# Gated attention with a routed mixture of experts: the expert table read along the pairs, first loads and transposes in front of the last attention products, three waits among GpSimd's last scatters

## The reference, cut to what matters

```python
x = L0_attn_x                       # 8 batches, 512 rows, 256 columns, float32
xn = _layernorm(x, axis=-1)
# attention over channels: scores are 256 x 256 per batch, summed over the 512 rows
scores = jnp.einsum('bes,bfs->bef', qT, kT) / np.sqrt(HEAD_DIM)
s = swapaxes(einsum(softmax(scores), vT)) @ Wo
# experts: 32, of 8 groups; the best 3 groups, in them the best 6 experts of each row
scores = jax.nn.softmax(xn @ gate_weight.T)
topk_weight, topk_idx = jax.lax.top_k(tmp_scores, TOP_K)      # TOP_K = 6
h = jax.nn.silu(xn @ w1[e].T) * (xn @ w3[e].T)                # for each expert e
y = sum over the chosen e of weight * (h @ w2[e].T)
shared = jax.nn.silu(xn @ sw1.T) * (xn @ sw3.T) @ sw2.T       # one expert for all rows
g = _silu(y + shared)
return x + s * g
```

## Time and profile before

| | |
|---|---|
| median of 3 runs | 695.25 us (692.28 to 696.24) |
| profiled execution, and its span | 693.48 us, 691.7 us |
| TensorE products busy | 543.7 us, 79% of the span |
| TensorE weight loads busy | 449.3 us, 65% |
| VectorE busy | 472.7 us, 68% |
| ScalarE busy | 357.0 us, 52% |
| GpSimd busy | 379.7 us, 55% |
| DMA | 174.80 MB, mean 253 GB/s |
| chain that ended last | DVE 32%, PE 27%, issue 18%, unknown queue 14% |

### The profile page before, as it was taken

The page is one execution under the profiler, slowest core; times in us unless marked ns, Lnnn a source line. Parts: engine busy times, 40 slices in busy tenths (PEclk is TensorE's granted clock), DMA queues, the critical chain, the costliest instruction groups (busy, mean ns, idle before and its releaser), DMA issues.

```text
span 691.7 us, 14479 instructions
## 1 busy us (share of the span) xinstructions
PE 543.7 (79%) x4095; PEld 449.3 (65%) x4095; DVE 472.7 (68%) x1443; ACT 357.0 (52%) x606; POOL 379.7 (55%) x402
## 2 busy tenths in 40 slices
PE   8778895979696859628999987878888788888840
PEld 7555774756565647427999776777767777677730
DVE  7966886888786848742454566767667677676767
ACT  5535573747464534324656554655646556465531
POOL 1275666766666667671003565656556565565664
PEclk9888997999998989777999999999999999999975
DMA  9999994949492523653998888998888889988765
GB/s 322 413 355 354 348 352 146 350 166 353 168 330 103 194 92 122 209 178 97 194 216 268 285 270 261 290 292 269 277 267 287 290 262 287 284 274 272 236 200 174
DMA packets 111288, 174.80 MB, mean 253 GB/s; under 512 B 25072, under 2 KB 68848, under 8 KB 110320
## 3 DMA queue, kind: packets, MB, share of 16 engines
q1 hardware_dynamic: 87280, 108.29, 47.9%
q0 software_dynamic: 18432, 50.36, 23.6%
q10 hardware_dynamic: 5504, 15.24, 6.2%
HBM read 78.41 MB, written 92.27 MB: 247 GB/s over the span
## 4 chain that ended last, share of the span: by engine, by line
DVE 32%; PE 27%; issue 18%; another core or an unknown queue 14%; ACT 7%; DVEq 1%; DMA 1%; ACTq 0%
DVE sw L1149 8%; PE ps L851 8%; PE ps L726 4%; PE ps L742 4%; DVE work L1175 3%; PE ps L873 3%; DVE w_all L1066 2%; DVE work L1168 2%; PE ps L748 2%; DVE early L1157 2%; PE ps L734 2%; PE ps L834 2%; DVE pad L1175 2%; ACT w_all L574 1%
## 5 line engine op out<-in xcount | busy, mean ns | idle before, releaser
L524 POOL DMA_INDIRECT early<-slots_d,slot_at x192 | 183.5, 956 | 186.6 <-remote 80.0
L503 POOL DMA_INDIRECT slots_d<-early,slot_at x96 | 97.5, 1015 | 70.9 <-issue 25.7
L503 POOL DMA_INDIRECT slots_d<-work,slot_at x96 | 96.5, 1006 | 45.8 <-issue 25.6
L663 ACT ACTIVATE xnT<-ps 128x1024 f16<-128x1024 f16 x67 | 68.9, 1029 | 86.0 <-remote 61.5
L834 PE MATMUL ps<-ident,work 128*128 128x128 f16 x796 | 70.6, 221 | 51.7 <-issue 51.6
L851 PE MATMUL ps<-w_all,xnT 128*128 x798 | 101.4, 276 | 3.6 <-issue 2.8
L834 PEld LDWEIGHTS ps<-ident,work 128*128 128x128 f16 x796 | 56.3, 99 | 58.8 <-issue 55.4
L851 PEld LDWEIGHTS ps<-w_all,xnT 128*128 128x128 f16 x798 | 73.4, 98 | 18.4 <-issue 8.1
L1175 DVE CAST work<-ps 128x256 f16<-128x256 f32 x75 | 31.7, 422 | 75.8 <-remote 53.3
L1149 DVE SCALAR_TENSOR_TENSOR sw<-early,wk,sw 128x256 f32<-128x256 f32 x160 | 77.8, 486 | 3.5
L684 ACT ACTIVATE early<-ps 128x512 f32<-128x512 f32 x112 | 67.9, 607 | 20.8 <-PE ps L873 10.7
(11 more groups left out here) (164 smaller groups left out, 968.2 us busy)
## 6 DMA issues: line engine op xcount, KB each, us to landing
slots_d<-early SPq DMA_DIRECT2D x112, 256.0 KB
work<-slots_d SPq DMA_DIRECT2D x100, 256.0 KB
slots_d<-pad SPq DMA_DIRECT2D x7, 3072.0 KB
w_all<-in_wexp ACTq DMA_DIRECT2D x7, 1536.0 KB
slots_d<-work SPq DMA_DIRECT2D x1, 5120.0 KB, 20.0
s_all<-in_x SPq DMA_DIRECT2D x8, 512.0 KB, 5.2
ysh_d<-work ACTq DMA_DIRECT2D x8, 512.0 KB
early<-ysh_d SPq DMA_DIRECT2D x32, 128.0 KB
```

Of the source, the lines that this page charges most:

```text
L503: pool.indirect_dma_start(slots_d[:, :], bass.IndirectOffsetOnAxis(ap=slot_at[:, at:at + 1], axis=0), split[b % XN_RING][:, t, :], None).t ...
L524: pool.indirect_dma_start(gath[:, at % GATH_RING, :], None, slots_d[:, :], bass.IndirectOffsetOnAxis(ap=slot_at[:, rank_of(at):rank_of(at) ...
L663: act.activation(x_halves[n % 3], turned_pair(p), ACT.Copy).then_inc(s_eT, 1)
```

## The change

What it does, part by part:

- **TensorE.** The table's transpose and the transposes of pair 0 (pair 1 is the DMA's) stand in front of the last attention products. Only six of the table's words are loaded ahead of the pairs; after that one word is loaded in each step from `turn_later(4)` on, 32 single loads.
- **ScalarE.** Pair 0's copy (`copy_turned(0)`) stands in front of the first copy of the attention's result.
- **VectorE.** The compare and the reduce of the page table become one instruction with an accumulated output. The page table comes first, then the low weights of experts 24 and 25, the table's row, the low weights of 26 and 27, then both low_weights_last. `full_pairs` runs one batch earlier.
- **SP.** The ready flags are loaded before the last raw weights are asked for, and the first pairs wait for the scatters of six batches instead of seven.
- **GpSimd.** In the last batch, scatter 18 no longer waits for the last attention products; scatter 16 waits for the copy of m, 18 for the table's row, 20 for all low weights.

```diff
@@ sync
+            sp.wait_ge(s_ready_at, 1)
+            ready = registers(nc, ENG.SP, ready_at, 0, EARLY, 2)
+            for k in range(XN_RING):
+                sp.wait_ge(s_disp[k], 16 * BATCH_ROWS * (B // XN_RING - 1))
+            sp.sem_inc(s_scattered, 1)
             sp.wait_ge(s_h, (B - 1) * HC + 1)
...
-            sp.wait_ge(s_disp[0], 16 * BATCH_ROWS * (B // 2))
-            sp.wait_ge(s_disp[1], 16 * BATCH_ROWS * (B // 2 - 1))
-            sp.sem_inc(s_scattered, 1)
-            sp.wait_ge(s_ready_at, 1)
-            ready = registers(nc, ENG.SP, ready_at, 0, EARLY, 2)
@@ gpsimd
-                       14: (s_m_ps, b + 1), 18: (s_at_ps, 2 * b + 2)}
+                       14: (s_m_ps, b + 1)}
                 if nxt:
...
+                else:
+                    due.update({16: (s_m, B), 18: (s_tables, 1), 20: (s_wlo, B * EB)})
@@ scalar
                 for n in range(2):
+                    if last:
+                        copy_turned(n)
                     act.wait_ge(s_at_ps, b * 2 + n + 1)
@@ tensor
+                if last:
+                    pe.wait_ge(s_ident16, 1)
+                    pe.wait_ge(s_table, 1)
+                    pe.transpose(ps[0:1, 5, 0:P], table[:], ident[:]).then_inc(s_table_ps, 1)
+                    turn_rows(0)
+                    turn_rows(1)
                 pe.wait_ge(s_m, b + 1)
...
             pe.wait_ge(s_tables, 1)
             pe.wait_ge(s_y, 2 * B)
-            half = WORDS // 2
-            packed = [word for at in (0, half)
-                      for word in registers(nc, ENG.PE, w_packed.bitcast(I32), at, half, (1 << 31) - 1)]
+            packed = list(registers(nc, ENG.PE, w_packed.bitcast(I32), 0, FIRST_WORDS, (1 << 31) - 1))
...
+            def turn_later(p):
+                if p >= 2:
+                    turn_rows(p)
+                if p >= 4 and len(packed) < WORDS:
+                    packed.extend(registers(nc, ENG.PE, w_packed.bitcast(I32), len(packed), 1, (1 << 31) - 1))
@@ vector
                         then(dve.tensor_scalar(at_or_under, ends[:, at:at + B * full // 2], tile_row[:, c:c + 1], None,
-                                               ALU.is_le))
-                        then(dve.tensor_reduce(gains[:, c, n:n + 1], at_or_under, AX_X, ALU.add))
+                                               ALU.is_le, ALU.add, accum_out=gains[:, c, n:n + 1]))
...
-                elif b + 2 == B:
+                if b + 3 == B:
                     full_pairs()
...
                 if b == B - 1:
-                    low_weights(b - 1)
                     page_table()
+                    low_weights(b - 1, range(HALF))
+                    table_row()
+                    low_weights(b - 1, range(HALF, EB))
                     low_weights_last(0)
-                    table_row()
                     low_weights_last(1)
                     return
```

More of the change, by code:

```diff
@@ L584, in gram, with copy_turned @@
                 act.activation(g_s, chunks(ps[:, 0, :]), ACT.Copy).then_inc(s_g, 1)
+            def copy_turned(p):
+                if not by_dma(p):
+                    n = turns(p) - 1
+                    if n >= 3:
+                        act.wait_ge(s_eab_ps, PE_PAIRS[n - 3] + 1)
+                    act.wait_ge(s_eT_ps, n + 1)
+                    act.activation(x_halves[n % 3], turned_pair(p), ACT.Copy).then_inc(s_eT, 1)
             def batch(b):
@@ L654, in _, with copy_later @@
                 batch(b)
[L657 to L663, removed]
+            def copy_later(p):
+                if p >= 2:
+                    copy_turned(p)
             def silu(p):
@@ L750, in gram, with loaded, turn_rows @@
                 mm.then_inc(s_g_ps, 1)
+            def loaded(p):
+                return 16 * sum(2 if by_dma(q) else 1 for q in range(p % DEEP, p + 1, DEEP))
+            def turn_rows(p):
+                if by_dma(p):
+                    return
+                if turns(p) >= 3:
+                    pe.wait_ge(s_eT, turns(p) - 2)
+                pe.wait_ge(s_slot[p % DEEP], loaded(p))
+                for low in range(2):
+                    for c in range(HC):
+                        for h in range(pages_in(p)):
+                            at = ((low * HC + c) * 2 + h) * P
+                            mm = pe.transpose(turned_pair(p)[:, at:at + P], slot16[:, at_slot(p) + h, low, c * P:(c + 1) * P],
+                                              ident16[:])
+                mm.then_inc(s_eT_ps, 1)
             def batch(b):
@@ L818, in weights_at @@
                 return ((word >> (16 * (n // 3) + FIELD * (n % 3))) & (E - 1)) * (2 * WEXP)
-            def loaded(p):
-                return 16 * sum(2 if by_dma(q) else 1 for q in range(p % DEEP, p + 1, DEEP))
-            def turn_rows(p):
-                if by_dma(p):
-                    return
-                if turns(p) >= 3:
-                    pe.wait_ge(s_eT, turns(p) - 2)
-                pe.wait_ge(s_slot[p % DEEP], loaded(p))
-                for low in range(2):
-                    for c in range(HC):
-                        for h in range(pages_in(p)):
-                            at = ((low * HC + c) * 2 + h) * P
-                            mm = pe.transpose(turned_pair(p)[:, at:at + P], slot16[:, at_slot(p) + h, low, c * P:(c + 1) * P],
-                                              ident16[:])
-                mm.then_inc(s_eT_ps, 1)
+            def turn_later(p):
+                if p >= 2:
+                    turn_rows(p)
+                if p >= 4 and len(packed) < WORDS:
+                    packed.extend(registers(nc, ENG.PE, w_packed.bitcast(I32), len(packed), 1, (1 << 31) - 1))
             def hidden(p):
@@ L876, in expert_out @@
                 mm.then_inc(s_ey_ps, 1)
-            in_steps((turn_hidden, 0, PAIRS), (expert_out, -LATE, PAIRS), (turn_rows, SOON + 2, PAIRS), (hidden, SOON, PAIRS))
+            in_steps((turn_hidden, 0, PAIRS), (expert_out, -LATE, PAIRS), (turn_later, SOON + 2, PAIRS), (hidden, SOON, PAIRS))
         @block.vector
@@ L1068, in low_part, with low_weights @@
                 ins.then_inc(s_wlo, 1)
-            def low_weights(b):
+            def low_weights(b, experts=range(EB)):
                 dve.wait_ge(s_whi, b + 1)
-                for e in range(EB):
+                for e in experts:
                     low_part(weights_of(b, 1)[:, e], raw_weights(b)[:, e], weights_of(b, 0)[:, e])
```

13 lines of the change are left out of this document (5 added, 8 removed).

## The result

The changed kernel took 701.53 us (median of 4 runs, 700.35 to 705.82) against 695.75 us (692.28 to 696.28) of the kernel before beside it: a ratio of 1.0106, 95% interval 1.0059 to 1.0153. It is slower by some 6 us; the prediction said 9 us faster, and gave slower a chance of 0.09.

What follows compares the result with a forecast made beforehand. No engine bounds the whole span; TensorE paces the pairs, so an earlier start ends earlier. 11.8 (start) - 3.7 (attention clock) + 2.0 (expert clock) - 1 = 9 us off the 695.25 median: 686.2, range 681.5 to 695.

Steps and rivals of the forecast that it cites:

- the sizing of the single loads: Pairs 4 to 23: TensorE's sequencer has 1.1 us a pair to spare, so a 0.116 us word costs 0.
- The second rival: Pairs 4 to 23: single loads of 1.6 to 2.2 us stop the array; slower from 0.45 us a pair; 702, chance 0.10.
- 11.8 - 3.7 = 8.1 us: Start of the pairs: first product 11.8 us earlier, less 3.7 for attention products at the lower clock.
- The added wait: Last batch: ScalarE's high weights wait for experts 24 to 27, delaying m and the attention products; alone costs 3.3 us.
- The six words: TensorE's register load ahead of the pairs: 0.7 us, hidden under the attention products.
- the line through zero: Register loads of 19 and 14 words: 0.116 and 0.115 us a word, no fixed part.
- the first rival: Last batch: the table's transpose is seen 5.3 us late, gain 5 to 8.5 us, priced at 690.3; chance 0.25.
- "Worth 0" for the later scatters: GpSimd's last scatters end at about 309, or 314 if five later, before SP needs them: 0 us.
- The clock on the first expert products (+2.0): First 24 expert products: 2.62 us at the higher clock instead of 4.67, about 2.0 us back.
- The fused form: VectorE's page table: compare and reduce in one instruction removes 4.1 us of reduces, but gives nothing by itself.
- The third rival: Pair stage gives the start back: 0 to 3 us of gain left, 693.5; chance 0.13.
- the 7.67 us of issue: Before pair 0's first transpose: two register loads of 19 words, 2.207 and 5.315 us.

Runs made afterwards that it cites:

- e2: The kernel before with the table's new place, six words loaded first, then pairs 4 to 35 one word each: 699.00 us, ratio 1.0057.
- e3: The changed kernel with the last six scatters held until pairs 0 to 5 are done, one after each: 699.03 us, ratio 1.0037.
- e9: The changed kernel with 16 loads of two words in place of the 32 of one: 704.51 us in one execution.
- e1: The changed kernel with the 38 words loaded in two loads of 19 ahead of the pairs: 695.42 us, ratio 0.9982.
- e4: The changed kernel with 12 words loaded first and the other 26 one by one from pair 26 on: 694.99 us, ratio 1.0002.
- e5: The changed kernel with 12 words first, the other 26 from pair 26 on, and the last six scatters held until pairs 0 to 5: 687.83 us, ratio 0.9897.
- e10: The kernel before with the table's new place, 12 words loaded first and 26 singly from pair 26 on: 700.09 us on a slower chip, ratio 0.9933.
- e6: e5 with VectorE making both halves of experts 24 to 27 before the table's row: 694.31 us on a slower chip, ratio 0.9877.

## Why the prediction was wrong

*The step that failed* is the sizing of the single loads: "Together 21 of 40 us, which leaves 1.1 us a pair. A word of 0.116 us fits; I take 0." Both halves were wrong. A single word takes 0.307 us, not 0.116. And the spare time was counted from the durations of the sequencer's records (46 ns, and 6 ns a hand-over taken from a burst behind a wait). In the running stage these records stand farther apart than they last. The trace of before had this in the prediction's own 40 us:

```profile
L873 PEldq FUSED_REGOPS  x4: 46/46/46, 346.8 to 347.2; - x4
```

The four start at 346.82, 346.95, 347.07 and 347.19, 0.124 us apart. In after the pace is the same right behind a load, where the array had run out of products (353.95, 354.07, 354.20), so the array doesn't set it. In the 40 us there are 194 such records at 0.124 us, 59 ALU operations at 0.097 and 59 waits at 0.106 or more: an estimate of some 36 of 40 us, not 21, which leaves 0.2 us a pair instead of 1.1. Between pairs 2 and 24 of after lie 22 single loads (the prediction counted about 20), which last 8.7 us together, some of them 0.5 to 0.8 us; 7.4 us of it show, 0.34 a load. In e2 it is 6.4 of 7.4 us, in e3 7.0 of 7.9, in e9 8.7 of 9.3. So nearly the whole load is exposed each time, and e1, e4 and e5 take it away (53.9, 53.5, 53.8 us against 53.6). The second rival named the place, and its time of 702 is what was measured, but by two errors that cancel: it had the loads cost 16 us and the start bring 9, and they cost 7.4 and the start brought 2.4. By its own point (0.45 us a pair, 9 in all) the loads alone would not have turned the change. Its price, 1.6 to 2.2 us a load, was not right either: one word took 0.31. The spare deserved a lower bound of zero, as every unknown does: TensorE at 40.00 of 40 says that the sequencer keeps up, not by how much.

*The start.* 11.8 - 3.7 = 8.1 us was forecast, measured from the batch's first scatter it is 9.5. The added wait worked as worked out: 1.48 us of high weights, then m, then the attention products, at 305.89 with 6.76 us for 3.72, at a granted clock of 0.50: 3.0 us more, where up to 3.7 was allowed. The six words took 1.22 us from 306.07, not 0.7, but under these products; the line through zero on which they were priced does not hold for short loads. What the sum lacked was when the first result is seen. Pair 0's silu came 36.8 us after the first scatter against 39.9 before: of 9.5 us, 3.1 were left. I had the effect in the first rival, with the right evidence, but hung it on the table's transpose alone. I asked "which result does the new chain hang on", and stopped at the first one. The same question at pair 0, with scatters ending at 309 to 314 in my own text, would have read: products at 304, seen 2 us after 309 to 314. "Worth 0" for the later scatters was the second wrong term. Where they are held, the silu comes 2.0 to 3.8 us after the first product's start; in the four kernels of the changed order that don't hold them (after, e1, e4, e9) it is 9.2, 7.6, 4.6 and 8.4. In time the cleanest comparison is e5 with e4, 0.9897 with 1.0002. That holding cures the loss is shown; why a result is seen late is not, and e2 and e10, in the order of before, saw pair 0's at once (2.8 and 2.2 us) under running scatters.

*The rest.* The clock on the first expert products (+2.0) is seen: at a granted clock of 0.99 (312 to 315 us) they take 1.47 us for 12, where before had 4.67 for 24. The fused form costs 0.75 + 0.08 us, under the compare and reduce it replaces (0.35 to 0.52 + 0.69), and like the rest of VectorE's table was off the path. The third rival is not seen: from pair 24 to the end it takes 315.6 us, before 314.8.

*Where the 7.67 us of issue went* was read rightly: the two loads. With them mended and the order left as it was, e10 gains 0.7%.

## What to carry to other kernels

A sequencer that feeds a full engine has its own budget: take the distance between its records in the running stage, not their length, and take the lead over the engine as zero until a gap in the engine's row shows it. Put scalar loads of this kind where the engine has slack; here 22 such loads cost 7 us between pairs 2 and 24, and 26 of them, behind pair 24, nothing that could be measured. When a start is moved forward, follow every result past it to the engine that waits for it, and ask what will be running then that was over before; a gain of 9.5 us and a new loss of 7.1 nearly cancelled here, and only running each cure alone and both together told them apart.

## What the runs showed of the hardware

- A register load by TensorE costs 0.30 to 0.32 us for one word in most cases (others up to 0.83, in e2 once 1.14), 0.54 for two in most, 1.02 to 1.22 for six in four traces and 1.04 to 1.25 for 12 in six (once 2.39): among running products a word is dear, in bulk cheap. Two loads of 19 took 2.0 to 2.4 and 4.5 to 5.3 us in three traces; why the second is slower by its double stays open. The Trainium skill (DMA: Bandwidth & Descriptors, Latency and other measured facts) has a floor of about 600 ns for such a load; the trace shows half of that.
- TensorE's results are at times seen late beside a stream of GpSimd's indirect DMAs: ScalarE waited 6.4 us in after, VectorE 12.2 in e4 and 10.4 in e6, with the release 0.1 us (e4's pair 0) to 2.8 us (e4's row) after GpSimd had stopped. With the last scatters held it did not occur at pair 0 in any of seven traces. But it is not a rule: in e2 and e10 the first product was seen at once beside running scatters. What tells the cases apart was not found, nor whether the result or only its signal is late, or whether the array itself runs later than recorded.
- The last batch's scatters start between 280.8 and 286.5 us into the span in kernels that are alike up to there, so the spans of two profiled executions can't carry a difference of 6 us. Short stretches between marks can: pair 2 to pair 24 takes 53.5 to 54.8 us in the ten traces without single loads there and 60.0 to 62.3 in the four with them. Long ones can't: pair 24 to the end scatters by 8 us.
